# Two attentions worked through by pairs of tiles instead of single tiles

## The reference

```python
# layer 0                                   # layer 1
q, k = elu(x@wq)+1, elu(x@wk)+1             q, k = rotate(x@Wq), rotate(x@Wk)
S = S + k[:, None]*v[None, :]   # causal    ret = (q @ k.T) * scaling * decay     # causal
y = (q @ S) / (q @ z + EPS)                 out = group_norm(ret @ v)
x = x + gate * (y @ w_proj)                 x = x + gate * ((silu(x@Wg) * out) @ Wo)
```

## Time and profile before

| what | value |
|---|---|
| median of 3 runs | 1028.99 us (1028.94 to 1034.72) |
| the profiled execution's own time | 1031.93 us |
| its span, first to last instruction | 1030.0 us |
| PE, DVE, ACT, POOL busy over the span | 83%, 83%, 60%, 72% |
| mean granted TensorE clock | 0.938 of full speed |
| kv product, 128 instructions on POOL | 264.0 us |
| states, 768 matmuls on PE | 263.4 us |
| products with q, 384 instructions on DVE | 180.6 us |

### The profile page before, as it was taken

The page is one execution under the profiler, slowest core; times in us unless marked ns, Lnnn a source line. Parts: engine busy times, 40 slices in busy tenths (PEclk is TensorE's granted clock), DMA queues, the critical chain, the costliest instruction groups (busy, mean ns, idle before and its releaser), DMA issues. The chain is left out here.

```text
span 1030.0 us, 22329 instructions
## 1 busy us (share of the span) xinstructions
PE 851.2 (83%) x5240; PEld 613.2 (60%) x5240; DVE 859.5 (83%) x2837; ACT 622.0 (60%) x1652; POOL 737.5 (72%) x642
## 2 busy tenths in 40 slices
PE   5699999999969968988888888559887623999993
PEld 5466666666637744555555555336655422999993
DVE  5589999999977966988898989779999761899995
ACT  1655555555429946676766666377764203999992
POOL 4488888888854528999999999574788461355554
PEclk9899999999989979999999999879999755999997
DMA  9420000000000000000000000264666564544420
GB/s 249 159 77 2 1 1 1 1 1 1 2 4 1 1 1 0 11 21 12 22 20 13 22 11 22 61 161 130 176 207 205 165 221 121 153 132 133 136 65 18
DMA packets 64978, 70.59 MB, mean 69 GB/s; under 512 B 8965, under 2 KB 52178, under 8 KB 64740
## 3 DMA queue, kind: packets, MB, share of 16 engines
q1 hardware_dynamic: 50612, 47.20, 16.5%
q0 software_dynamic: 6368, 16.89, 4.8%
q10 hardware_dynamic: 7872, 5.08, 1.9%
HBM read 32.32 MB, written 24.50 MB: 55 GB/s over the span
## 5 line engine op out<-in xcount | busy, mean ns | idle before, releaser
L473 PE MATMUL a_pS<-a_kv,utri 128*128 128x360 f32 (+3 forms) x768 | 263.4, 479 | 12.9 <-POOL a_kv L464 11.0
L464 POOL TENSOR_TENSOR a_kv<-a_qk,a_vv 128x1152 f32<-128x1152 f32 (+1 forms) x128 | 264.0, 2063 | 12.6 <-DVE a_qk L438 12.6
L473 PEld LDWEIGHTS a_pS<-a_kv,utri 128*128 128x128 f32 x768 | 136.4, 191 | 91.5 <-POOL a_kv L464 25.8
L569 POOL TENSOR_TENSOR a_tt<-a_tt 128x576 f32<-128x576 f32 (+1 forms) x128 | 156.8, 1225 | 41.1 <-DVE a_tt L553 40.6
L553 DVE TENSOR_TENSOR a_tt<-a_pS,a_qk 128x360 f32<-128x360 f32 (+3 forms) x384 | 180.6, 525 | 4.9 <-PE a_pS L473 4.9
L1950 POOL DMA_INDIRECT out_dram<-x_o,x_place x71 | 69.2, 975 | 75.6 <-DVE x_o L1937 74.6
L519 ACT ACTIVATE a_tt<-a_pI 128x144 f32<-128x144 f32 (+1 forms) x96 | 40.0, 417 | 108.3 <-PE a_pI L481 108.2
L581 DVE TENSOR_REDUCE a_nd<-a_tt 128x144 f32<-128x720 f32 (+3 forms) x128 | 104.4, 816 | 0.0
L1530 POOL DMA_INDIRECT ys<-m_S,m_dest x64 | 63.2, 988 | 36.4 <-issue 12.8
L512 PEld LDWEIGHTS a_pO<-wgate,a_yT 128*128 128x128 f32 x256 | 44.6, 192 | 74.5 <-POOL a_yT L543 50.2
L512 PE MATMUL a_pO<-wgate,a_yT 128*128 128x128 f32 x256 | 54.7, 296 | 30.0 <-POOL a_yT L543 21.2
(11 more groups left out here) (299 smaller groups left out, 2194.0 us busy)
## 6 DMA issues: line engine op xcount, KB each, us to landing
x_yl<-ys SPq DMA_DIRECT2D x71, 193.5 KB, 2.4
X<-xs SPq DMA_DIRECT2D x16, 256.0 KB, 4.8
kx<-m_kc SPq DMA_DIRECT2D x64, 64.0 KB
ax<-m_pc SPq DMA_DIRECT2D x64, 64.0 KB
m_S<-X SPq DMA_DIRECT2D x16, 256.0 KB, 2.8
xs<-X SPq DMA_DIRECT2D x15, 256.0 KB
w<-in_L_ffn_W_dram SPq DMA_DIRECT2D x1, 2048.0 KB
m_S<-gw ACTq DMA_DIRECT2D x6, 256.0 KB, 3.2
```

The lines of the kernel that those rows point to most:

```text
L464: pool.tensor_tensor(kv[:, t % 2, :, :, :], kk.unsqueeze(2).to_broadcast([P, H, J, D]), vv[:, t, :, :].unsqueeze(3).to_broadcast([P, H, J, ...
L473: pe.matmul(pS[c][:, 0:(h1 - h0) * SC], K.utri[:, :], flat[:, h0 * SC:h1 * SC], start=True, stop=True).then_inc(u_done, 1)
L569: pool.tensor_tensor(tt[:, t % 2, :, :, D // 2:D], tt[:, t % 2, :, :, D // 2:D], tt[:, t % 2, :, :, 0:D // 2], ALU.add).then_inc(half_done, 1)
```

## The change

Loops over single tiles become steps over pairs. A step is (b, u): batch b, tiles 2u and 2u+1 (ta and tb). In each step an engine also issues work of the pairs one to four steps back and of the pair ahead.

- One instruction for a pair in place of two: `pool_kv`, `pool_halve`, `pool_rope`, `pool_gate`, `vec_den`, `vec_var`, `vec_rec`, `vec_y`, `vec_residual`, `act_square`, `act_sd`, and in layer 1 `act_yT`. `kv` and `tt` now hold four tiles, `y` and `yT` two; q and k are laid out as two blocks of four tiles. Everything else stays one instruction a tile.
- The order within a step is written out engine by engine, for each layer apart (`pe_step`, `act_step`, `vec_step`, `pool_step`). y of a pair is made two steps after its products, projection and residual follow three after, statistics four after. The odd tile's q and k are made first thing in the next DVE step; rows are normalised a tile sooner.
- The three results in the bank `pI` change places, and a transpose into it waits until ACT has read what was put there before.
- In layer 1 the gate has three slots instead of two, in memory that held layer 0's projection weights, and the table for the square root is loaded right after Silu.

Cut to what is spoken of below (the PE and ACT steps are in the same style):

```diff
-        kv = sb("kv", [P, 2, H, J, D])
-        tt = sb("tt", [P, 2, H, J, D + 1])
+        kv = sb("kv", [P, TPB, H, J, D])
+        tt = sb("tt", [P, TPB, H, J, D + 1])
...
+        def pool_kv(pool, b, u):
+            n, t = 2 * b + u, 2 * u
+            pool.wait_ge(qk_ready, qk_count(b, t + 1))
+            pool.wait_ge(v_ready, 4 * b + t + 2)
+            wait(pool, u_done, 6 * (n - 1))
...
+            pool.tensor_tensor(kv[:, t:t + 2, :, :, :].rearrange("p t h j i -> p (t h) j i"),
+                               kk.unsqueeze(2).to_broadcast([P, 2 * H, J, D]),
+                               rows.unsqueeze(3).to_broadcast([P, 2 * H, J, D]), ALU.mult).then_inc(kv_ready, 1)
...
+        def pe_project(pe, b, u):
+            n = 2 * b + u
+            pe.wait_ge(yT_ready, 2 * n + 2 if layer == 0 else n + 1)
+            wait(pe, x_done, n)
+            pe.wait_ge(y_ready, min(n + 2, NP) if isinstance(b, int) else n + 2)
...
+        def pool_halve(pool, b, u):
+            n, t = 2 * b + u, 2 * u
+            pool.wait_ge(t_done, 6 * n + 6)
+            two = lambda i: tt[:, t:t + 2, :, :, i:i + D // 2].rearrange("p t h j i -> p (t h) j i")
+            pool.tensor_tensor(two(D // 2), two(D // 2), two(0), ALU.add).then_inc(half_done, 1)
...
+            act.activation(gate[slot], pT[:, :], ACT.Silu).then_inc(gate_ready, 1)
+            act.preload_act_table_set("sqrt_and_others")
```

The end of `act_step` in layer 1:

```diff
+                if last:
+                    act_sd(act, *last)
+                if back:
+                    act_yT(act, *back, 1)
+                if cur and u == 0 and more:
+                    act_gate(act, b + 1, (phase + 1) % 3)
```

`vec_step` in layer 0, cut in its middle (between, products, a sum, the first state and the even tile's q and k):

```diff
+        def vec_step(v, b, u):
...
+            cur, last, ready = pair(b, u, 0), pair(b, u, -1), pair(b, u, -2)
+            out, done = pair(b, u, -3), pair(b, u, -4)
+            late = last and known(last[0], 1) and (last[0] + 1, 2 * last[1] + 1)
+            if layer == 0:
+                if late:
+                    vec_qk(v, *late)
+                if done:
+                    vec_stats(v, *done, 1)
+                if ready:
+                    vec_y(v, *ready)
+                if cur:
+                    vec_product(v, b, ta, 0)
+                    vec_product(v, b, ta, 1)
...
+                if last:
+                    vec_sum(v, last[0], 2 * last[1] + 1)
+                if out:
+                    vec_residual(v, *out)
+                if last:
+                    vec_den(v, *last)
+                if cur and tb < 3:
+                    vec_state(v, b, tb)
+                if last:
+                    vec_rec(v, *last)
```

`pool_step` in layer 1:

```diff
+                if last:
+                    pool_halve(pool, *last)
+                if ahead:
+                    pool_rope(pool, *ahead)
+                if out:
+                    pool_gate(pool, *out, (phase + (u - 3) // 2) % 3)
+                if ahead:
+                    pool_kv(pool, *ahead)
```

More of the change, by code:

```diff
@@ L328, in attention @@
             rb = sb("rb", [P, 2, 2 * P])
[L329 to L333, removed]
+            gate = [K.wgate[:, 0, 4 * s:4 * s + 4, :].rearrange("p a f -> p (a f)") for s in range(3)]
+            sq = sb("sq", [P, 2, P])
+            vs = sb("vs", [P, 2 * H])
+            sd = sb("sd", [P, 2 * H])
+            yaff = sb("yaff", [P, 2 * P])
             wqkv = K.W[:, W_Q1:W_V1 + 1, :].rearrange("p a b -> p (a b)")
@@ L497, in pe_transpose_y @@
[L497 to L501, removed]
[L502 to L513 removed]
+            wait(pe, qT_ready, 3 * b + t - 1)
@@ L515, in act_inter @@
+        def pe_project(pe, b, u):
[3 more added lines that the diff above has]
+            pe.wait_ge(y_ready, min(n + 2, NP) if isinstance(b, int) else n + 2)
+            for k in range(2):
+                mm = pe.matmul(pO[:, k * P:(k + 1) * P], yT[:, k, :], tile(K.wgate[:, 0 if layer == 0 else 2, :, :], b),
+                               start=True, stop=True)
+            mm.then_inc(proj_ps, 1)
         def act_inter(act, b, t):
@@ new lines, in vec_step @@
+                if cur and tb < 3:
+                    vec_state(v, b, tb)
+                if last:
+                    vec_rec(v, *last)
+            else:
+                if late:
+                    vec_qk(v, *late)
+                if ready:
+                    vec_rec(v, *ready)
+                if cur:
+                    vec_product(v, b, ta, 0)
+                if ready:
+                    vec_y(v, *ready)
+                if cur:
+                    vec_product(v, b, ta, 1)
+                    vec_product(v, b, ta, 2)
+                    vec_state(v, b, ta)
+                if last:
+                    vec_sum(v, last[0], 2 * last[1])
+                    vec_sum(v, last[0], 2 * last[1] + 1)
+                if cur and more:
+                    vec_qk(v, b + 1, ta)
+                if cur:
+                    vec_product(v, b, tb, 0)
+                    vec_product(v, b, tb, 1)
+                    vec_product(v, b, tb, 2)
+                if out:
+                    vec_residual(v, *out)
+                if last:
+                    vec_var(v, *last)
+                if cur and tb < 3:
+                    vec_state(v, b, tb)
@@ new lines, in pool_step @@
+        def pool_step(pool, b, u, phase):
+            last, out, ahead = pair(b, u, -1), pair(b, u, -3), pair(b, u, 1)
+            if layer == 0:
+                if last:
+                    pool_halve(pool, *last)
+                if ahead:
+                    pool_kv(pool, *ahead)
+            else:
+                if last:
+                    pool_halve(pool, *last)
+                if ahead:
+                    pool_rope(pool, *ahead)
+                if out:
+                    pool_gate(pool, *out, (phase + (u - 3) // 2) % 3)
+                if ahead:
+                    pool_kv(pool, *ahead)
@@ L802, in _ @@
                     finish_stats_vector(v, K, var_ready, std_ready, rstd_ready, 1, slice(0, 8))
-                if layer == 0:
-                    for n in range(NT - 4, NT):
-                        tile_stats(v, K, K.X, n, bn_done)
             @block.gpsimd
```

516 lines of the change are left out of this document (284 added, 232 removed).

## The result

| | before | after |
|---|---|---|
| median | 1030.03 us (4 runs, 1028.94 to 1034.72) | 997.85 us (4 runs, 997.22 to 999.7) |
| span of the profiled execution | 1030.0 | 997.9 |
| ratio | | 0.968, 95% interval 0.965 to 0.972 |

What follows compares the result with a forecast made beforehand. DVE was taken to pace layer 0 and POOL layer 1, with PE beside DVE in layer 0 afterwards. Layer terms -13.2 and -18.4 gave -31.6, from 1031.9 to 1000.3, then 2.9 lower for the median: 997 us, range 984 to 1019.

Steps and rivals of the forecast that it cites:

- The total: Both layers together: -31.6 us, from -13.2 in layer 0 and -18.4 in layer 1, giving 997 us.
- Layer 0's period: Layer 0, time per pair of tiles: from 7.70 to 7.15 us, PE and DVE side by side at 7.0.
- The ends: Layer 0's start and end: 2.5 us lost at the start and 1.9 at the end, 4.4 in all.
- Layer 1's period: Layer 1, time per pair, paced by POOL: from 8.42 to 7.75 us, pairing its four instructions saving 0.75.
- halving's waits: POOL in layer 1: halving still waits for a product now and then, so 7.75 a pair instead of 7.67.
- Layer 1's start and end: Layer 1: about 3 us gained in the first step, 6 lost (5 to 7) before the statistics at the end.
- First rival: POOL's charge grows with width and pairing saves nothing, layer 1 staying at 8.42 a pair: 1019 us, chance 0.10.
- Second rival: Layer 0: PE and DVE wait for each other's products in lockstep, losing the 0.55 a pair: 1015 us, chance 0.13.
- Third rival: Layer 1: ACT's 3.2 us block of table loads and gate delays the next v copy: 1045 us, chance 0.08.
- 0.8 of slack: Layer 1: DVE's room against POOL before a late v copy costs time, each further microsecond paid once per batch.
- The rows named ahead: POOL's paired instructions, expected durations in us: kv 4.19 and 3.74, halving 2.36 and 2.12, rope 1.27, gate 0.73.
- v-copy wait: Layer 1: a wait of DVE's rope for the v copy once a batch would show the ACT block.

Runs made afterwards that it cites:

- e0: The changed kernel run once more, unedited, as the base of the runs beside it: 999.45 us, ratio 0.967.
- e1: Changed kernel with each of POOL's four pair instructions (kv, halving, rope, gate) issued as two of half the width: 1016.95 us, ratio 0.986.
- e2: Changed kernel with DVE's pair instructions (residual, y, denominator, reciprocal, variance sum) issued as two of half the width: 1000.92 us, ratio 0.971.
- e4: Changed kernel with two more ACT table loads behind each Silu gate of layer 1: 1031.61 us, ratio 0.999.
- e10: Changed kernel with every second pair's layer 1 gate on DVE, and layer 1's end reordered with fewer stores ahead of the read-back: 987.48 us, ratio 0.958.

## Why the prediction was right, point by point

- **The total** is right in part by luck, because two errors cancel. Layer 0 was forecast at -13.2 and gave 265.8 - 249.2 = -16.6; layer 1 was forecast at -18.4 and gave -14.9 (-16.7 in e0). Together -31.5 (-32.6 in e0) against -31.6.
- **Layer 0's period**: PE at 6.99 and DVE at 6.96, "7.15, 2% for waits on each other". PE measured 7.00, DVE 6.88, and the waits did not come: PE was busy throughout. The step that failed is that 2%. DVE was a little better than priced: denominator and reciprocal take 0.50 a pair in the mean where 0.56 was taken. The forecast's reason, that the reciprocal is followed at once by other work, holds; but in every second step it still stands right behind its denominator, and waits for it. The ends lost 32 x 0.70 - 16.6 = 5.8, forecast 4.4.
- **Layer 1's period**: 7.71 against 7.75, by a saving that was mis-sized. 0.75 was read from durations; a duration holds some 0.05 in which the next row has begun (483.62 + 1.96 against 485.53). By starts the saving is 0.57 (e1 gives 0.49), and 0.2 came from halving's waits, which the forecast kept.
- **Layer 1's start and end** were the worst terms. Forecast were 3 gained at the start; from the stage's start to its first kv 8.9 against 9.5 before, and the last kv to the last product 1.6 against 1.9 (each less one period), so 0.9 was gained. At the end, the residual 7.6 after the last product, forecast 7.2; the statistics 15.9 in e0, forecast 14 to 15; 7.0 lost against 6, and 8.7 with the slow transfer.
- **First rival** (POOL charges by width alone): fell to e1. 14 to 16 us of layer 1 hang on it. The Trainium skill's 2.6 cycles an element (GPSIMD Engine Reference, 3.1), from which pairing would have given next to nothing, does not fit the kv rows here: their starts grow by 1.72 ns a column, with 0.15 us fixed.
- **Second rival** (lockstep in layer 0): fell; in 150 us no wait of PE's matmuls or of DVE on the other shows, and PE's weight loads waited 1.9 us in all for DVE's products. e2 shows that it is not far off: 0.16 more on DVE put 0.09 on the period. The Trainium skill (Perfetto Trace Analysis, Optimizing Scalar/DVE Operations) says, of ScalarE and VectorE, that grouping can pay where the engine is saturated. The trace has the same of POOL, on both sides: splitting POOL again cost layer 1, where it runs without a gap, 14 to 16 us, and layer 0, where it waits, nothing.
- **Third rival** (ACT's block): did not happen, by 0.3 to 0.45 us a batch. The forecast gave "0.8 of slack" and one for one from there; if the second holds, which e4 fits but does not show alone, the slack was half of the first. A chance of 0.08 was low for so small a margin.
- **The rows named ahead**: kv 4.16 and 3.77 (said 4.19 and 3.74), halving 2.39 and 2.20 (2.36 and 2.12), rope 1.33 (1.27), gate 0.78 (0.73). The v-copy wait that was to show the ACT block is there, 4.5 in 160 us, but once a step and not once a batch, at most 0.2, and free: it is for the odd tile's copy, which stands ahead of the block. The copy behind the block ends at 493.25, and the rope that needs it starts at 493.28 without a wait printed.

## What to carry to other kernels

Price a queue that runs without a gap from start to start, not by durations: the fixed part saved by a wider instruction came out 0.13 to 0.15 that way, and 0.16 to 0.21 by durations. Pairing pays on the engine that paces (0.5 of 8.2 a pair on POOL, nothing on the same instructions in layer 0), and dependent small instructions issued for two tiles together pay even at the old widths (0.59 of 7.70). Then follow the last tiles to whoever waits for them: doubled steps lengthen the drain, and reordering it, with half of the gate (0.35 us a pair) moved from the pacing engine to the next, was worth another 12 us.

## What the runs showed of the hardware

- POOL's durations vary between executions while the distances of its starts do not: means of kv, halving, rope and gate are 3.77, 2.19, 1.33 and 0.79 us after the change and 3.72, 2.14, 1.27 and 0.73 in e4, where POOL waits 22 of 160 us. All four differ by the same 0.05 to 0.06, and from start to start, without a wait, rope takes 1.23 and halving 2.09 to 2.10 in both.
- While PE waits at the end of layer 1, its clock falls: 1.00 granted from 600 to 616, a mean of 0.75 from 616 to 626, where it is busy 4.5 of 10 us, and 0.50, the lower level of 1.2 GHz, from 626 to 636. The same four matmuls of a projection then take twice as long (timeline of PE, after):

```profile
616.06 0.61 PE L536 MATMUL a_pO<-wgate,a_yT 128*128 128x128 f32 x4
...
623.91 1.22 PE L536 MATMUL a_pO<-wgate,a_yT 128*128 128x128 f32 x4 [2.22 <-POOL a_yT L569]
```

That is 0.6 us in the chain to the second-last pair's residual.
- The 64 KB store took 3.3 us from its issue to the read-back's in the first profile of the changed kernel, 2.1 in e10 and 1.7 in all others. In the two slow ones a packet of the queue `instruction` (16 KB in 1.28 us, 8 KB in 0.65) runs while the store's packets move, and some of these start only when it has ended; in the others it comes before or after them. That the packets waited for it is read from these times alone.
